# A graph layer's accumulator adds, taken from PSUM through an SBUF copy that ScalarE makes

## The chip, the cores and the metric

One core of one Trainium2 chip. The metric is the device time of one execution in microseconds (us), the median of several runs. Five engines work side by side, each through its own queue in order: TensorE (PE in the profile, its weight loads PEld), VectorE (DVE), ScalarE (ACT), GpSimd (POOL) and SyncE (SP). They meet by semaphores only.

## What is computed

```python
# x (6250, 64); src, dst, edge_type (200000,), edges sorted by dst; weight (16, 64, 64)
h = maximum(layernorm(x), 0)
msg[e] = h[src[e]] @ weight[edge_type[e]]
x + segment_sum(msg, dst, num_segments=6250)
```

## The kernel before

The result is summed in SBUF, transposed, in one wide tile: `accT`, one column for each of the 6250 nodes, the 64 features twice over the 128 partitions (the two halves are added at the very end). Edges are sorted by target, so a stretch of edges touches a window of at most 32 nodes, and its sum is added into 32 columns of `accT` that begin at a base read from the data (`base_row`).

The edges take two ways to a window:

- 125440 of them in 140 groups of 896, worked on two at a time: 70 pairs, n = 0 to 69. For a pair TensorE gathers source rows by products with one-hot matrices (L1264), ScalarE copies the gathered rows from PSUM to SBUF (`take_messages`, L672), and TensorE sums them by relation and target (L1281) into banks 3 and 4. `take_sums` (L681) copies those two banks to `agg`. For every second pair `weigh` (L1308) multiplies the sums of four groups by the 16 weight matrices: 4 windows of 32 columns in one bank, the target bank.
- 74560 of them in 98 stretches of at most 768. GpSimd fetches ready products `h @ weight` from a table in DRAM, and `sum_gathered` (L1324) sums each stretch into 32 more columns of the same target bank.

Batch k (k = 1 to 35) is one filled target bank: 128 columns from `weigh(k - 1)` and 32 for each of its gathered stretches (three in most batches, two in four of them, none in the last). Bank 5 holds odd batches, bank 7 even ones, so a bank is written again two batches later.

`add_sums(k)` on VectorE empties it: a load of four bases into registers (L974), a wait for the weighing (`s_fl`) and for the last gathered sum (`s_sump`), four adds, a load of the other bases (L985), and an add for each gathered stretch, all at L966, each waiting for the one before (`s_add`). It reads the bank where it lies, in PSUM. Before batch k, `weigh` and `sum_gathered` wait until the adds of batch k - 2 are done (`added_by(k - 2)`).

The order is written out by hand. On TensorE a pair has three steps c = 0, 1, 2 (a third of its gathers each), and in each step the gathers come first and then the sums (L1281) of the step before. In step 0 of an even pair n this gives: gathers; the last sums of pair n - 1; gathered stretches; `sort_permute` (L1173). Step 1: gathers; `rank_spilled` (L1181), which waits for `z_sb`; sums of step 0; `weigh` of batch n/2. ScalarE in step 0: `take_messages`, `take_sums(n - 1)`, `take_z` (L615, which fills `z_sb`), and then `take_messages` of step 1. VectorE in pair n: `sort_slots(n + 2)` (L818, L820, L812), `sort_values` (L858), `sort_ranges`, `source_hots` (L936), in even pairs `add_sums(n/2 - 1)`, then `key_hots` (L946) of the next pair, in a ring of 22 buffers that TensorE's sums set free, with `sort_spilled` (L832, L812) and more between them.

After the last pair ScalarE does `take_sums(69)`, TensorE `weigh(34)`, and VectorE, in the branch that is taken when no window overflows, `last_sums`: `add_sums(34)` and `add_sums(35)`. Then it signals `s_done` (L1070), TensorE turns `accT` back (L1387), and VectorE adds the halves and x (L1081).

Of the kernel before, what the change touches and what calls it, by code (L numbers as in the profile page):

```python
# [11 lines left out]
ALU = mybir.AluOpType  # L12
ACT = mybir.ActivationFunctionType
AX = mybir.AxisListType.X
P = 128
EPS = 1e-5
BANK = 512
# [12 lines left out]
def gnn_program(nc, x, src, dst, etype, weight, out):  # L30
# [11 lines left out]
    NS, SJ, SQ, SK, SW, GR = 140, 7, 17, 3, 32, 4  # L42
# [4 lines left out]
    NPR, PT = NS // 2, 2 * SJ  # L47
# [12 lines left out]
    PJ, PW, PRING, PHOTS = 6, 32, 8, 6  # L60
# [114 lines left out]
    for i in range(FETCHES):  # L175
        at = FIRST + (LAST - FIRST) * i / FETCHES
        four = i - len(tile_time)
        spills = four < NGR and starts[2 * four + 1] <= at or len(tile_time) == PALL
        at = max(at, starts[2 * four + 1]) if spills else at
# [14 lines left out]
    batch = [place[m] // 2 for m in range(NP)]  # L194
    batches = [[m for m in range(NP) if batch[m] == k] for k in range(NPR // 2 + 1)]
    adds_of = lambda k: GR * (k >= 1) + len(batches[k])
    added_by = lambda k: sum(adds_of(i) for i in range(k + 1))

    def target_bank(k):
        return ps[(7, 5)[k % 2]]  # L200

    def sum_place(m):
        at = GR * SW + batches[batch[m]].index(m) * PW
        return slice(at, at + PW)
# [18 lines left out]
    sb = lambda name, shape, dt=F32: ctx.enter_context(nc.sbuf_tensor(name, shape, dt))  # L223
    sem = lambda name: ctx.enter_context(nc.semaphore(name))
    with ctx:
# [27 lines left out]
        spreadv = sb("spreadv", [P, PT, 2, SQ], F16)  # L253
        z_sb = sb("z_sb", [P, 3, 2, SQ])
        rel_row = sb("rel_row", [SQ, 2, P], F16)
        iota_key = sb("iota_key", [P, R * SW], F16)
        iota_slot = sb("iota_slot", [P, P], F16)
        iota_range = sb("iota_range", [P, SQ], F16)
# [26 lines left out]
        at = 0  # L285
# [8 lines left out]
        for name in ("src_p", "typ_p", "dst_p"):  # L294
# [48 lines left out]
        s_hot, s_khot, s_gat, s_gev, s_agg, s_aev, s_fl, s_add = (  # L343
            sem(f"s_{n}") for n in ("hot", "khot", "gat", "gev", "agg", "aev", "fl", "add"))
        s_gp = [sem(f"s_gp{k}") for k in range(PRING)]
        s_hotp, s_sump, s_go = sem("s_hotp"), sem("s_sump"), sem("s_go")
        s_over = sem("s_over")
        s_src_b, s_typ_b, s_dst_b, s_nat_b, s_turn_b, s_turned_b, s_base_b, s_row_b = (
            sem(f"s_{n}") for n in ("src_b", "typ_b", "dst_b", "nat_b", "turn_b", "turned_b", "base_b", "row_b"))
        s_done, s_oT, s_half, s_res = sem("s_done"), sem("s_oT"), sem("s_half"), sem("s_res")  # L350
# [208 lines left out]
        def _(act):  # L559
# [58 lines left out]
            def take_rel(g):  # L618
                act.wait_ge(s_relT, g + 1)
                if g >= 2:  # L620
                    act.wait_ge(s_rel[g % 2], 16 * (g // 2))
                act.copy(rel_row[:, g % 2, :], ps[6][0:SQ, 0:P]).then_inc(s_relrow, 1)

            def take_spilled(g):

                act.wait_ge(s_xz, g + 1)
                w = g // 2
                if w >= 2:
                    act.wait_ge(s_xwin, w - 1)
                act.copy(spill_z[:, w % 2, :], ps[6][:, 480:488]).then_inc(s_xzev, 1)  # L630
# [33 lines left out]
            def take_messages(n, c):  # L664
                for b in banks_of(n, c):
                    u = n * GB + b
                    act.wait_ge(s_gat, u + 1)
                    if u >= MB:
                        last_n, last_b = divmod(u - MB, GB)
                        act.wait_ge(s_agg, last_n * SQ + min(2 * last_b + 2, SQ))  # L670
                    width = min(2, SQ - 2 * b)
                    act.copy(msg_s[:, u % MB, 0:width, :].rearrange("p q c -> p (q c)"),  # L672
                             ps[gather_bank(u)][:, 0:width * ROW]).then_inc(s_gev, 1)

            def take_sums(n):
                act.wait_ge(s_agg, (n + 1) * SQ)
                g = n // 2
                if g >= 1:
                    act.wait_ge(s_fl, g)
                for a in range(2):  # L680
                    act.copy(agg[:, n % 2 * 2 + a, :], ps[3 + a][:, :]).then_inc(s_aev, 1)  # L681

            for n, c in STREAM:
                take_messages(n, c)
                if turned(n, c):
                    take_rel(turned(n, c))
                if spilled(n, c) and spilled(n, c) % 2 == 1:
                    take_spilled(spilled(n, c))
                if c == 2 and n in (TURN_AT, KEY_TURN_AT):
                    take_last((TURN_AT, KEY_TURN_AT).index(n))  # L690
                if c == 0 and n >= 1:
                    take_sums(n - 1)
                if permuted(n, c):
                    take_z(permuted(n, c))
            take_sums(NPR - 1)

            def general(act):
                for n, (a, b) in enumerate(gbanks):
# [8 lines left out]
        def _(dve):  # L707
# [249 lines left out]

            def add_sums(k):

                bank = target_bank(k)  # L960

                def add(rows, base, width, at):
                    if added[0]:
                        dve.wait_ge(s_add, added[0])
                    here = accT[rows, bass.ds(base, width)]
                    dve.tensor_tensor(here, here, bank[rows, at], ALU.add).then_inc(s_add, 1)  # L966
                    added[0] += 1

                if k == 1:
                    dve.wait_ge(s_acc0, 8)  # L970
                    dve.wait_ge(s_row_s, 16)
                if (k - 1) * GR == NSA:
                    dve.wait_ge(s_row_b, 16)
                _, bases = nc.values_load_multi_w_load_instructions(  # L974
                    base_row[0:1, (k - 1) * GR:k * GR], engines=[dve.engine], min_val=0, max_val=N,
                    skip_runtime_bounds_check_because="the bases are clamped to it where they are made")
                dve.wait_ge(s_fl, k)
                if batches[k]:
                    dve.wait_ge(s_sump, batches[k][-1] + 1)
                for i, base in enumerate(bases):  # L980
                    add(slice(0, P), base, SW, slice(i * SW, (i + 1) * SW))
                if batches[k]:
                    if batches[k][0] == 0:
                        dve.wait_ge(s_row_p, 16)
                    _, bases = nc.values_load_multi_w_load_instructions(  # L985
                        base_row[0:1, NS + batches[k][0]:NS + batches[k][-1] + 1], engines=[dve.engine], min_val=0, max_val=N,
                        skip_runtime_bounds_check_because="the bases are clamped to it where they are made")
                    for m, base in zip(batches[k], bases):
                        add(slice(0 if len(tiles_of(m)) > 1 else tiles_of(m)[0] % 2 * D, P), base, PW, sum_place(m))
# [12 lines left out]
            for n in range(NPR):  # L1002
# [8 lines left out]
                if n % 2 == 0 and n >= 4:  # L1011
                    add_sums(n // 2 - 1)
# [59 lines left out]
            for g, (a, b) in enumerate(out_groups):  # L1072
                dve.wait_ge(s_oT, g + 1)
                for half in range(2):
                    for i in range(a, b, OB // 2):
                        n = min(b - i, OB // 2)
                        bank = ps[g % 4 * 2 + (i - a) // (OB // 2)][:, 0:n * P].rearrange("p (t h d) -> p t h d", h=2, d=D)
# [9 lines left out]
        def _(pe):  # L1087
# [211 lines left out]
            def weigh(g):  # L1299
                k = g + 1  # L1300
                pe.wait_ge(s_aev, (g + 1) * GR)
                if added_by(k - 2) > 0:
                    pe.wait_ge(s_add, added_by(k - 2))
                pe.wait_ge(s_gx[g % 2], 16 * (g // 2 + 1))
                pe.wait_ge(s_xwin, g + 1)
                for r in range(R):
                    half, first = r % 2, r < 2
                    last = pe.matmul(target_bank(k)[half * D:(half + 1) * D, 0:GR * SW], w_cat[:, r, :], agg[:, :, r * SW:(r + 1) * SW],  # L1308
                                     start=first, stop=r >= R - 2)
                    if r < R - 1:  # L1310
                        spot(last)
                    if r == R // 2 - 1:
                        pe.matmul(target_bank(k)[0:D, 0:GR * SW], msg_x[:, g % 2, :], win_x[:, g % 2, :], start=False, stop=False)
                last.then_inc(s_fl, 1)

            def sum_gathered(m):
                pe.wait_ge(s_hotp, m + 1)
                pe.wait_ge(s_gp[m % PRING], 16 * fetched(m))
                if added_by(batch[m] - 2) > 0:
                    pe.wait_ge(s_add, added_by(batch[m] - 2))  # L1320
                tiles = tiles_of(m)
                for j in tiles:
                    rows, half = rows_of(m, j), j % 2
                    last = pe.matmul(target_bank(batch[m])[half * D:(half + 1) * D, sum_place(m)], msg_p[rows, m % PRING, j, :],  # L1324
                                     hot_p[rows, m % PHOTS, j, :], start=j < tiles[0] + 2, stop=j >= PJ - 2)
                last.then_inc(s_sump, 1)
# [55 lines left out]
            for g, (a, b) in enumerate(out_groups):  # L1382
                if g >= 4:
                    pe.wait_ge(s_res, g - 3)
                for t in range(a, b):
                    bank, i = ps[g % 4 * 2 + (t - a) // (OB // 2)], (t - a) % (OB // 2)
# [17 lines left out]
```

## Time and profile before

| | |
|---|---|
| Time, median of 3 runs | 1066.32 us (1064.34 to 1066.62) |
| Profiled execution, first to last instruction | 1203.7 us |
| TensorE matmuls busy | 1083.9 us (90%) |
| VectorE busy | 938.3 us (78%) |
| GpSimd busy | 682.1 us (57%) |
| ScalarE busy | 450.0 us (37%) |
| Mean granted TensorE clock | 0.984 |

The profiled execution has no time of its own beside its span, and the span is 137.4 us longer than the median without the profiler. So a share of the span is not a share of the time, and TensorE's busy time is by itself more than the median. Durations are read from the profile; differences are added to the median.

In rows of a timeline a group of the same instructions is merged: start, us from the first start to the last end, and the count. In square brackets stands how long the engine was idle before, and who ended that. "remote" and "another core or an unknown queue" are releasers that the profile does not know; "issue" is none at all.

### The profile page before, as it was taken

How to read it: one execution, taken by the hardware profiler on the slowest of the kernel's cores; microseconds unless marked ns; L12 is line 12 of the kernel's file. 1: busy time of each engine (PE TensorE's matmuls, PEld its weight loads, DVE VectorE, ACT ScalarE, POOL GpSimd, SP SyncE). 2: the span in 40 equal slices, each digit the busy share in tenths (PEclk: the TensorE clock that was granted, in tenths of full speed). 3: DMA queues.
4: the chain of work that ended last, by engine and by line, in shares of the span. 5: the costliest groups of instructions: out<-in, count | busy, mean ns of one | idle time of the engine just before them, and what ended most of it. 6: DMA issues, size and time to landing. Idle time of an engine off the chain costs nothing.

```text
span 1203.7 us, 39145 instructions
## 1 busy us (share of the span) xinstructions
PE 1083.9 (90%) x15421; PEld 740.5 (62%) x15421; DVE 938.3 (78%) x2773; ACT 450.0 (37%) x1157; POOL 682.1 (57%) x647
## 2 busy tenths in 40 slices
PE   3998999899989889999999999999999999999897
PEld 1445666666666566666666666666666666666665
DVE  7756878897877688788778778878887887888874
ACT  4884333333333333333333333333333333333332
POOL 2213665566666665667666666666665656666630
PEclk9998999999999899999999999999999999999999
DMA  6795222222222122222222122222222222222211
GB/s 173 301 401 186 59 61 59 58 59 59 62 59 59 37 57 59 59 60 58 59 58 57 43 59 58 60 59 58 60 59 60 59 58 59 58 60 59 59 32 56
DMA packets 41739, 93.69 MB, mean 78 GB/s; under 512 B 14572, under 2 KB 14574, under 8 KB 41557
## 3 DMA queue, kind: packets, MB, share of 16 engines
q1 hardware_dynamic: 13850, 42.12, 10.3%
q0 software_dynamic: 19776, 20.29, 9.9%
q10 hardware_dynamic: 7930, 28.76, 6.2%
q8 instruction: 126, 2.06, 0.7%
q14 instruction: 57, 0.46, 0.1%
HBM read 63.52 MB, written 27.59 MB: 76 GB/s over the span
## 4 chain that ended last, share of the span: by engine, by line
PE 74%; issue 8%; DVE 6%; ACT 5%; another core or an unknown queue 3%; DMA 2%; ACTq 1%; POOL 0%; SPq 0%; DVEq 0%; POOLq 0%
PE ps L1281 33%; PE ps L1264 21%; PE ps L1308 6%; PE ps L1324 3%; ACT u L602 3%; PE ps L1173 3%; DVE u L946 2%; PE ps L1164 2%; PE ps L1197 2%; DMA table<-u 1%; DMA w_cat<-weight 1%; PE ps L1158 1%; PE ps L1203 1%; PE ps L1186 1%
## 5 line engine op out<-in xcount | busy, mean ns | idle before, releaser
L529 POOL DMA_INDIRECT u<-table,row_idx x583 | 612.7, 1051 | 411.3 <-PE ps L1264 138.8
L1281 PE MATMUL ps<-u 64*64 64x512 bf16 (+1 forms) x7280 | 466.5, 377 | 18.0 <-issue 16.0
L672 ACT CAST u<-ps 128x384 bf16<-128x384 f32 (+1 forms) x630 | 265.2, 465 | 527.8 <-PE ps L1264 464.2
L946 DVE TENSOR_SCALAR u<-iota_key,z_sb 128x512 bf16<-128x512 f16 x1190 | 359.9, 368 | 70.3 <-PE ps L1281 50.9
L1264 PE MATMUL ps<-parts,u 128*128 128x192 bf16 x3430 | 333.6, 250 | 11.0 <-issue 9.3
L1281 PEld LDWEIGHTS ps<-u 64*64 64x64 bf16 x7280 | 215.0, 106 | 204.7 <-issue 75.9
L1264 PEld LDWEIGHTS ps<-parts,u 128*128 128x128 bf16 x3430 | 280.6, 99 | 41.0 <-issue 38.5
L936 DVE TENSOR_SCALAR u<-u,node_id 128x1152 bf16<-128x1152 f16 (+2 forms) x420 | 184.5, 495 | 0.0
L681 ACT COPY u<-ps 128x512 f32<-128x512 f32 x140 | 75.2, 589 | 109.5 <-remote 76.8
L966 DVE TENSOR_TENSOR accT<-accT,ps 128x32 f32 x238 | 44.8, 188 | 58.4 <-DVE accT L966 23.1
L1308 PE MATMUL ps<-u,w_cat 128*64 128x128 f32 x1120 | 77.4, 277 | 1.7 <-ACT u L681 1.2
L812 DVE TENSOR_TENSOR u<-iota_slot,rank 128x896 f16<-128x896 f16 x70 | 76.4, 1092 | 2.4
L832 DVE SCALAR_TENSOR_TENSOR spill_rank<-ps,spill_mask 128x14 f32<-128x14 f32 x70 | 11.7, 167 | 84.1 <-issue 30.1
L1308 PEld LDWEIGHTS ps<-u,w_cat 128*64 128x64 f32 x1120 | 65.5, 136 | 15.9 <-issue 14.3
L1324 PE MATMUL ps<-u 128*64 128x32 f32 x1166 | 58.2, 226 | 15.4 <-issue 15.2
L1324 PEld LDWEIGHTS ps<-u 128*64 128x64 f32 x1166 | 46.2, 137 | 38.6 <-issue 37.5
L516 POOL DMA_INDIRECT msg_x<-table,spill_row x35 | 48.2, 1377 | 34.4 <-PE ps L1264 19.2
L1115 PE MATMUL ps<-w_cat,hT 64*128 64x512 f32 x196 | 62.7, 670 | 2.7 <-ACT u L602 2.6
L1173 PE MATMUL ps<-spreadv,u 128*128 128x68 f16 x490 | 30.0, 197 | 27.3 <-DVE spreadv L858 13.2
L602 ACT COPY u<-ps 128x512 f32<-128x512 f32 x98 | 50.7, 604 | 7.6 <-PE ps L1115 3.4
L812 DVE TENSOR_TENSOR spill_hot<-iota_slot,spill_rank 128x448 f16<-128x448 f16 x70 | 43.9, 627 | 2.4
L858 DVE TENSOR_TENSOR spreadv<-ranges,vals 128x476 f16<-128x476 f16 x70 | 45.5, 650 | 0.0
(131 smaller groups left out, 656.4 us busy)
## 6 DMA issues: line engine op xcount, KB each, us to landing
u<-rel_dram SPq DMA_DIRECT2D x70, 544.0 KB
table<-u ACTq DMA_DIRECT2D x24, 1024.0 KB, 5.2
u<-table,row_idx POOLq DMA_INDIRECT x583
rel_dram<-rel_row SPq DMA_DIRECT2D x70, 4.2 KB
x_sb<-x SPq DMA_DIRECT2D x2, 448.0 KB
out<-h_sb SPq DMA_DIRECT2D x3, 224.0 KB
out<-h_sb ACTq DMA_DIRECT2D x3, 224.0 KB
msg_x<-table,spill_row POOLq DMA_INDIRECT x35
```

Of the source, the lines that this page charges most:

```text
L529: pool.indirect_dma_start(out=msg_p[:, b, j, :], out_offset=None, in_=table, in_offset=bass.IndirectOffsetOnAxis(ap=row_idx[:, j, m:m + 1] ...
L602: act.copy(t_out[:, i % TRING, t, half * BANK:(half + 1) * BANK], ps[piece_bank(k)][:, :]).then_inc(s_tev, 1)
L672: act.copy(msg_s[:, u % MB, 0:width, :].rearrange("p q c -> p (q c)"), ps[gather_bank(u)][:, 0:width * ROW]).then_inc(s_gev, 1)
L681: act.copy(agg[:, n % 2 * 2 + a, :], ps[3 + a][:, :]).then_inc(s_aev, 1)
L812: return dve.tensor_tensor(there, places, mine, ALU.is_equal)
L936: last = dve.tensor_scalar(hot[:, part % HRING, k, 0:(there - low) * P], bc[:, b, low * P:there * P], node_id[:, k:k + 1], None, ALU.is_equal)
L946: dve.tensor_scalar(khot[:, v % KR, :], iota_key[:, :], z_sb[:, n % 3, 1, q:q + 1], None, ALU.is_equal).then_inc(s_khot, 1)
L1173: last = pe.matmul(ps[6][:, 0:4 * SQ].rearrange("p (a c) -> p a c", a=2), slot_hot[:, j, :], values[:, :, j, :], start=j == 0, stop=j == S ...
L1264: last = pe.matmul(there, hot[:, part % HRING, t - q * SK, at * P:(at + 1) * P], parts[:, t, :], start=t == blocks[0], stop=t == blocks[-1])
L1281: last = pe.matmul(ps[3 + a][half * D:(half + 1) * D, keys], msg_s[rows, u % MB, q % 2, part * D:(part + 1) * D], khot[rows, v % KR, keys] ...
L1308: last = pe.matmul(target_bank(k)[half * D:(half + 1) * D, 0:GR * SW], w_cat[:, r, :], agg[:, :, r * SW:(r + 1) * SW], start=first, stop=r ...
L1324: last = pe.matmul(target_bank(batch[m])[half * D:(half + 1) * D, sum_place(m)], msg_p[rows, m % PRING, j, :], hot_p[rows, m % PHOTS, j, : ...
```

## The change

ScalarE gets `take_targets(k)`: it waits for the weighing and for the gathered sums of batch k and for VectorE's adds of batch k - 2, and copies the used columns of the target bank to a new SBUF tile with two halves, `target_sb`. It stands behind `take_sums(n - 1)` in even pairs from n = 4 on, ahead of `take_z`, and twice at the end. `add_sums` waits for that copy (`s_kept`) alone and reads `target_sb`. `weigh` and `sum_gathered` wait for the copy of batch k - 2, no longer for its adds.

```diff
+        target_sb = sb("target_sb", [P, 2, BANK])
...
+            def take_targets(k):
+
+                act.wait_ge(s_fl, k)
+                if batches[k]:
+                    act.wait_ge(s_sump, batches[k][-1] + 1)
+                if added_by(k - 2) > 0:
+                    act.wait_ge(s_add, added_by(k - 2))
+                width = GR * SW + len(batches[k]) * PW
+                act.copy(target_sb[:, k % 2, 0:width], target_bank(k)[:, 0:width]).then_inc(s_kept, 1)
...
                 if c == 0 and n >= 1:
                     take_sums(n - 1)
+                    if n % 2 == 0 and n >= 4:
+                        take_targets(n // 2 - 1)
                 if permuted(n, c):
                     take_z(permuted(n, c))
             take_sums(NPR - 1)
+            take_targets(NPR // 2 - 1)
+            take_targets(NPR // 2)
...
-                bank = target_bank(k)
+                kept = target_sb[:, k % 2, :]
...
-                    dve.tensor_tensor(here, here, bank[rows, at], ALU.add).then_inc(s_add, 1)
+                    dve.tensor_tensor(here, here, kept[rows, at], ALU.add).then_inc(s_add, 1)
...
-                dve.wait_ge(s_fl, k)
-                if batches[k]:
-                    dve.wait_ge(s_sump, batches[k][-1] + 1)
+                dve.wait_ge(s_kept, k)
...
             def weigh(g):
                 k = g + 1
                 pe.wait_ge(s_aev, (g + 1) * GR)
-                if added_by(k - 2) > 0:
-                    pe.wait_ge(s_add, added_by(k - 2))
+                if k > 2:
+                    pe.wait_ge(s_kept, k - 2)
...
-                if added_by(batch[m] - 2) > 0:
-                    pe.wait_ge(s_add, added_by(batch[m] - 2))
+                if batch[m] > 2:
+                    pe.wait_ge(s_kept, batch[m] - 2)
```

What ScalarE has in a row in step 0 of an even pair, before. L672 copies gathered rows, L681 is `take_sums`, L615 `take_z` (line numbers of after are 2 higher up to here):

```order
L672 CAST u<-ps 128x384 [waits s_agg,s_gat] x3
L681 COPY u<-ps 128x512 [waits s_fl,s_agg]
L681 COPY u<-ps 128x512
L615 COPY z_sb<-ps 64x34 [waits s_relT,s_khot,s_z]
L615 COPY z_sb<-ps 64x34
L672 CAST u<-ps 128x384 [waits s_agg,s_gat] x3
```

And now:

```order
L674 CAST u<-ps 128x384 [waits s_agg,s_gat] x3
L683 COPY u<-ps 128x512 [waits s_fl,s_agg]
L683 COPY u<-ps 128x512
L693 COPY target_sb<-ps 128x224 [waits s_add,s_sump,s_fl]
L617 COPY z_sb<-ps 64x34 [waits s_relT,s_khot,s_z]
L617 COPY z_sb<-ps 64x34
L674 CAST u<-ps 128x384 [waits s_agg,s_gat] x3
```

The copy, of 224 columns here (30 of the 35 have 224, four have 192, the last has 128), stands between `take_sums` and `take_z`; nothing else moved.

ScalarE's end, after the gathers of the last pair, before:

```order
L672 CAST u<-ps 128x384 [waits s_agg,s_gat] x5
L672 CAST u<-ps 128x192 [waits s_agg,s_gat]
L681 COPY u<-ps 128x512 [waits s_fl,s_agg]
L681 COPY u<-ps 128x512
L363 TENSOR_LOAD flag_int [waits s_flag]
```

And now:

```order
L674 CAST u<-ps 128x384 [waits s_agg,s_gat] x5
L674 CAST u<-ps 128x192 [waits s_agg,s_gat]
L683 COPY u<-ps 128x512 [waits s_fl,s_agg]
L683 COPY u<-ps 128x512
L693 COPY target_sb<-ps 128x224 [waits s_add,s_sump,s_fl]
L693 COPY target_sb<-ps 128x128 [waits s_add,s_fl]
L365 TENSOR_LOAD flag_int [waits s_flag]
```

Both last copies stand behind the last `take_sums`; the load of the flag follows them.

VectorE's end, before: the last three adds of batch 34, the load of the bases of batch 35, and its first adds, which wait for the weighing.

```order
L985 TENSOR_LOAD base_row
L966 ISA [waits s_add]
L966 TENSOR_TENSOR accT<-accT,ps 128x32
L966 ISA [waits s_add]
L966 TENSOR_TENSOR accT<-accT,ps 128x32
L966 ISA [waits s_add]
L966 TENSOR_TENSOR accT<-accT,ps 64x32
L974 TENSOR_LOAD base_row
L966 ISA [waits s_add,s_fl]
L966 TENSOR_TENSOR accT<-accT,ps 128x32
```

And now:

```order
L999 TENSOR_LOAD base_row
L982 ISA [waits s_add]
L982 TENSOR_TENSOR accT<-accT,target_sb 128x32
L982 ISA [waits s_add]
L982 TENSOR_TENSOR accT<-accT,target_sb 128x32
L982 ISA [waits s_add]
L982 TENSOR_TENSOR accT<-accT,target_sb 64x32
L990 TENSOR_LOAD base_row
L982 ISA [waits s_add,s_kept]
L982 TENSOR_TENSOR accT<-accT,target_sb 128x32
```

The order is the same; the adds of batch 35 wait for ScalarE's copy, and so do those of batch 34 above them (`s_kept` in place of `s_fl` and `s_sump`).

## Rows read from the trace of the kernel before

**Rows 1.** The page's busy times: us, share of the span, instructions.

```profile
PE 1083.9 (90%) x15421; PEld 740.5 (62%) x15421; DVE 938.3 (78%) x2773; ACT 450.0 (37%) x1157; POOL 682.1 (57%) x647
```

**Rows 2.** The page's chain that ended last, by engine.

```profile
PE 74%; issue 8%; DVE 6%; ACT 5%; another core or an unknown queue 3%; DMA 2%; ACTq 1%; POOL 0%; SPq 0%; DVEq 0%; POOLq 0%
```

**Rows 3.** Groups by line, columns: busy us, mean ns; idle us before, releasers.

```profile
L966 DVE TENSOR_TENSOR accT<-accT,ps 128x32 f32 x238 | 44.8, 188 | 58.4 <-DVE accT L966 23.1 <-PE ps L1308 8.5 <-issue 2.6
L1308 PE MATMUL ps<-u,w_cat 128*64 128x128 f32 x1120 | 77.4, 277 | 1.7 <-ACT u L681 1.2 <-issue 0.3
```

**Rows 4.** The same view, shapes apart: ScalarE's copies from PSUM.

```profile
L681 ACT COPY u<-ps 128x512 f32<-128x512 f32 x140 | 75.2, 589 | 109.5 <-remote 76.8 <-PE ps L1281 32.5
L595 ACT COPY hT<-ps 128x128 f32<-128x128 f32 x24 | 6.6, 278 | 9.9 <-PE ps L1115 6.1 <-PE ps L1109 3.7
```

**Rows 5.** The same view, VectorE: a PSUM operand, then SBUF operands alone.

```profile
L818 DVE TENSOR_TENSOR ranks<-ps,ranges 128x238 f32<-128x238 f32 x70 | 27.8, 397 | 14.0 <-PE ps L1164 10.6 <-remote 2.9 <-DVE win_x L848 0.2
L842 DVE TENSOR_TENSOR spill_terms<-spill_z,spill_coef 128x16 f32<-128x16 f32 x35 | 6.1, 174 | 13.7 <-issue 8.5 <-ACT spill_z L630 5.0
L847 DVE CAST spill_row<-spill_sum 128x1 int32<-128x1 f32 x35 | 5.4, 153 | 1.2
```

**Rows 6.** Timeline of ScalarE, step 0 of an even pair: start, us, what.

```profile
638.39 1.07 ACT L681 COPY u<-ps 128x512 f32<-128x512 f32 x2 [1.96 <-remote]
639.35 0.40 ACT L615 COPY z_sb<-ps 64x34 f32<-64x34 f32 x2
639.77 1.24 ACT L672 CAST u<-ps 128x384 bf16<-128x384 f32 x3
```

**Rows 7.** TensorE in the same place: the last gathers, and who waits.

```profile
639.16 0.33 PE L1264 MATMUL ps<-parts,u 128*128 128x192 bf16 x2 [0.22 <-issue]
639.80 0.18 PE L1181 MATMUL ps<-spill_mask,tri 128*128 128x14 f16 x1 [0.31 <-ACT z_sb L615]
```

**Rows 8.** Waits: TensorE for z_sb, in all 70 pairs: us, times, longest.

```profile
PEld ps L1181 <- ACT z_sb L615: 19.2, 29, 1.2
PE ps L1181 <- ACT z_sb L615: 11.1, 22, 1.0
```

**Rows 9.** Timeline of ScalarE, the even pair before: the same two lines.

```profile
606.81 1.07 ACT L681 COPY u<-ps 128x512 f32<-128x512 f32 x2 [2.06 <-remote]
607.77 0.39 ACT L615 COPY z_sb<-ps 64x34 f32<-64x34 f32 x2
```

**Rows 10.** Timeline of VectorE from there to its next sort.

```profile
607.69 1.14 DVE L966 TENSOR_TENSOR accT<-accT,ps 128x32 f32 x4
609.57 0.83 DVE L966 TENSOR_TENSOR accT<-accT,ps 128x32 f32 x3 [0.73 <-DVE accT L966]
...
611.84 0.63 DVE L812 TENSOR_TENSOR spill_hot<-iota_slot,spill_rank 128x448 f16<-128x448 f16 x1
...
617.76 1.81 DVE L946 TENSOR_SCALAR u<-iota_key,z_sb 128x512 bf16<-128x512 f16 x6 [2.29 <-PE ps L1281]
```

**Rows 11.** TensorE there: end of the gathers in step 1; next gathers; spill_hot's reader.

```profile
608.65 0.17 PE L1181 MATMUL ps<-spill_mask,tri 128*128 128x14 f16 x1
...
613.48 1.25 PE L1264 MATMUL ps<-parts,u 128*128 128x192 bf16 x13
614.65 0.38 PE L1197 MATMUL ps<-vals,spill_hot 128*64 128x8 f16 x7
```

**Rows 12.** Timeline of VectorE's end: batch 34, and then batch 35.

```profile
1178.22 0.51 DVE L966 TENSOR_TENSOR accT<-accT,ps 128x32 f32 x2 [2.49 <-PE ps L1324]
...
1181.36 0.19 DVE L966 TENSOR_TENSOR accT<-accT,ps 64x32 f32 x1 [0.16 <-DVE accT L966]
1190.06 1.15 DVE L966 TENSOR_TENSOR accT<-accT,ps 128x32 f32 x4 [8.51 <-PE ps L1308]
```

**Rows 13.** The other engines there, in order of time.

```profile
1186.60 1.07 ACT L681 COPY u<-ps 128x512 f32<-128x512 f32 x2 [3.08 <-PE ps L1281]
...
1188.82 1.09 PE L1308 MATMUL ps<-u,w_cat 128*64 128x128 f32 x15
```


## What the change should do to the time

> **What bounds the kernel now.** Four views, in this order. The busy times [rows 1]: TensorE's matmuls 90% of the span, VectorE 78%, ScalarE 37%. The chain that ended last [rows 2] runs through TensorE for 74%, VectorE 6%, ScalarE 5%. So TensorE sets the pace, and VectorE is near: its 938.3 us are 88% of the 1066.32 us that an execution takes without the profiler. The groups by line [rows 3] show what the change touches: 238 adds of 188 ns, 44.8 us, and idle time before them of 58.4 us, of which 23.1 is one add waiting for another (register loads lie between) and 8.5 the last batch waiting for the weighing. No wait of an add for the weighing or the gathered sums shows in the loop. `weigh` was idle for 1.7 us in all, and for no add of VectorE. So the wait of TensorE that the change shortens, for batch k - 2, holds nobody up today: by the order of work it lies two even pairs back. The last views are timelines of step 0 of an even pair and of the end.
>
> **The copy's size.** A copy of 512 fp32 columns from PSUM takes 589 ns on ScalarE, one of 128 takes 278 [rows 4]: 0.81 ns a column. One of 224 then takes some 356 ns. Behind another copy it adds less: two of 512 end after 1.07 us [rows 6], so the second adds 0.48, and one of 224 columns adds 0.48 - 288 x 0.81 = 0.25 us. 35 copies are some 12 us on an engine that is busy for 450 of 1203.7. ScalarE's own waits in it are over when it comes there: the weighing of the batch and all its gathered sums stand ahead of this pair's gathers on TensorE, and VectorE's adds of batch k - 2 two even pairs back.
>
> **Who stands behind the copy on ScalarE.** First `take_z`, and for that TensorE waits (L1181). [Rows 6, 7] show an even pair in which this is tight: `take_sums` 638.39 to 639.46, z from 639.35 to 639.75, TensorE goes on at 639.80 after 0.31 us of waiting. Put 0.25 us between the first two and TensorE is 0.25 us later. [Rows 9, 11] show the pair before: z ends at 608.16, TensorE comes at 608.65, and the 0.25 us are covered. I went through the 32 even pairs in which the loop has both: in 7 (the first at 165.3, the last at 1012.9) it is as in [rows 6, 7]; in 7 others z directly follows `take_sums`, but TensorE is over 0.4 us later; in the rest z waits for `sort_permute` on TensorE or comes long before it is wanted, so that the copy fits in ahead or goes unseen. 7 x 0.25 = **1.7 us** on TensorE's path. Ends: nothing, if TensorE is always later than z, and 32 x 0.36 = 11.5 us if every pair is tight and the copies don't overlap. I take 1.7, since it is counted. How often TensorE waits for z in all 70 pairs [rows 8] (29 and 22 times, 30.3 us) says that this edge is sharp. Next in ScalarE's queue are the copies of step 1's gathers; TensorE wants those banks again at 613.48 [rows 11], 4 us after they are free, so nothing comes of it.
>
> **What VectorE loses.** (a) The adds. Nothing makes them shorter. A two-tensor operation with a PSUM operand takes 397 ns for 238 columns [rows 5] and 188 for 32 [rows 3], so 1.01 ns a column; one with SBUF operands alone takes 174 for 16 columns [rows 5], and 16 columns more make it 190. 238 x 2 ns is 0.5 us, on an engine with slack. The Trainium skill (VectorE: DVE Perf Modes, the section on the TRN2 errata) has a table in which an operation from PSUM has 62 cycles more of fixed cost than one from SBUF; by it the adds would be 65 ns shorter, 15 us in all. The same section says that a fixed term of some 150 cycles is what was measured for fp32 adds from SBUF; these rows side with that. (b) The wait. Before, adds began as soon as VectorE came to them. Now they need the copy: the end of `take_sums`, 0.25 us for the copy, and 0.15 from one engine to the next (as from TensorE's end at 1189.91 to the add at 1190.06 [rows 12, 13]). In [rows 9, 10] `take_sums` ends at 607.88 and the adds began at 607.69: now 608.28, 0.59 us later. Over the 33 batches in the loop the same sum gives a wait in 21, 15.2 us together, at most 1.9. Behind it in VectorE's queue are the key matrices of the next pair and the sort of spilled edges. The latter's product is at 612.47 and is wanted at 614.65 [rows 10, 11]: 2.2 us of cover. Then VectorE stands still for 2.29 us, until TensorE frees a buffer of the ring [rows 10]. Such a gap before its next sort follows in all but two of these batches, as long as the new wait or within 0.1 us of it. So in this trace the wait is hidden: **0**. Ends: 0 and 15.2 us.
>
> **The end of the program.** Here nothing hides it. Before, batch 34 is added from 1178.22 to 1181.55, under TensorE's last work, VectorE then waits 8.51 us, and batch 35 is added from 1190.06 to 1191.21 [rows 12]. Now the copy of batch 34 stands behind the last `take_sums`, which ends at 1187.67 [rows 13]. Copy: 1187.92; first add: 1188.07. Seven adds with the register load between take 2.71 us in the loop [rows 10]: 1190.78. The load of batch 35's bases, hidden in the 8.51 us so far, takes the 0.73 that such a load shows [rows 10]: 1191.51. The copy of batch 35 is no limit: weighing ends at 1189.91 [rows 13], plus 0.28 and 0.15 is 1190.34. Four adds, 1.15: 1192.66, against 1191.21. **1.45 us**. Ends: 0.7 if the load overlaps the adds before it, 2.1 if batch 34 takes the 3.33 us that it took in [rows 12].
>
> **Sum.** 1.7 + 0 + 1.45 = 3.1 us, and no gain against it. On the median: 1066.32 + 3.1 = **1069.4 us**. The profiled span is 137 us longer than that median, but the terms are lengths of instructions on ScalarE and VectorE and a count of tight places; the count is what may differ without the profiler. Something under 0.2% (2.1 us) can't be told from no change here.
>
> **Rivals.**
> A, only the end counts. In half the even pairs `take_sums` begins some 2 us after the sums that it needs, released by something the profile doesn't know [rows 6, 9]. If that is due to the profiler, ScalarE is earlier in a timed run, z waits for `sort_permute` instead, and the copy costs TensorE nothing. Against it: TensorE is quicker too. The time is 1066.3 + 1.45 = 1067.8, no change that can be told.
> B, VectorE's wait comes through. It holds if VectorE has no slack left in a timed run, which its 88% suggests [rows 1]. Against it: a VectorE that is late comes to the adds after the copy, and then there is no wait. Half of 15.2 with the 3.1 gives 1077.
> C, faster: VectorE is what the timed run waits for, and the adds do get shorter. The floor for an operation from SBUF is the 153 ns of a one-column cast [rows 5]: 35 ns less for each of 238 is 8.3 us. With the end's 1.45 that is 1059.5. It decides for faster from (2.1 + 1.45) / 238 = 15 ns an add. The slope above speaks against it. The table of the Trainium skill named above points this way.
> That the change does nothing is excluded: the new order has the copies and the waits on both sides.
>
> **Chances.** As worked out (1068 to 1072): 0.42, of it 0.07 under 2.1 us. A: 0.27. B: 0.15. C: 0.07. Other: 0.09, a third each way. That makes slower 0.35 + 0.15 + 0.03 = 0.53, same 0.07 + 0.27 + 0.03 = 0.37, faster 0.07 + 0.03 = 0.10. The range leaves out C and the far half of B: 1065 to 1076.5.
>
> **What would show it.** In the profile of after: 35 copies of about 356 ns; TensorE's idle time at `rank_spilled`, for z, up by about 2 us; adds of 188 to 191 ns; idle time before the loop's adds up by about 15 us, for ScalarE's copy, and idle time of the key matrices, for TensorE, down by as much; the last add ending some 2.7 us after TensorE's last weighing matmul, where it was 1.3 [rows 12, 13]. I am wrong if the adds are under 175 ns, if TensorE's idle time for VectorE's sorts (L1173) rises, or if batch 34 at the end is not added behind the last `take_sums`.

## The result

The median of 20 runs is 1067.61 us (1065.09 to 1070.41), against 1065.62 us (1063.58 to 1068.45) for 20 runs of the kernel before. The ratio is 1.0022, with a 95% interval of 1.0011 to 1.0032: 2.3 us slower, between 1.2 and 3.4. (The ratio is not that of the two medians, which lie 2.0 us apart; here and below the microseconds come from the ratio.) Forecast were 3.1 us, 1069.4 us in all; the time lies in the range of 1065 to 1076.5, and just under the 1068 to 1072 of the case as it was worked out.

One thing must be said ahead of the profile. Its span is 1068.1 us, where that of before was 1203.7 us. This is not the change's doing. The runs were on several chips, on which the kernel before takes 1065, 1181 to 1183 and 1199 us *without* the profiler. By its span the profile of before comes from a chip of the long kind (over 1180 us); the times of before come from one of the short kind (1065 us). The prediction took the difference for the profiler's. That it is the chip and not its host, say, was not tested. So the two profiles can't be laid side by side in the loop; in the end they can, since nothing waits there for what is late on the long chips. For the loop the experiments give the profile that is wanted: one kernel whose loop is that of before, on the short kind.

The page of after, its busy times (us, share of the span, instructions), as [rows 1], and its chain, as [rows 2]:

```profile
PE 1010.9 (95%) x15421; PEld 709.7 (66%) x15421; DVE 937.4 (88%) x2773; ACT 469.7 (44%) x1192; POOL 687.2 (64%) x647
...
PE 63%; DVE 22%; issue 7%; ACT 4%; DMA 3%; DVEq 1%; ACTq 1%; POOL 0%; SPq 0%; POOLq 0%
```

VectorE's busy time is what it was, in a span 136 us shorter, and it now holds 22% of the chain. The groups by line (busy us, mean ns, idle us before, releasers), as [rows 3, 4]:

```profile
L982 DVE TENSOR_TENSOR accT<-accT,target_sb 128x32 f32 x238 | 45.9, 193 | 61.3 <-DVE accT L982 24.9 <-ACT target_sb L693 13.5 <-issue 1.1
L683 ACT COPY u<-ps 128x512 f32<-128x512 f32 x140 | 75.2, 589 | 91.4 <-PE ps L1295 91.4
```

238 adds of 193 ns in place of 188: not shorter, but 5 ns longer. They wait 13.5 us for ScalarE's copy, but in the list of waits (us, times, longest) this is nearly one wait, of 12.9 us, at the end; and TensorE hardly waits for z, against [rows 8]:

```profile
DVE accT L982 <- ACT target_sb L693: 13.5, 2, 12.9
...
PEld ps L1195 <- ACT z_sb L617: 1.5, 2, 0.8
```

The copies themselves (duration ns least, median, most):

```profile
L693 ACT COPY target_sb<-ps x35: 266/363/365, 159.6 to 1051.9; 128x224 f32<-128x224 f32 x30, 128x192 f32<-128x192 f32 x4, 128x128 f32<-128x128 f32 x1
```

An even pair of the loop, timeline of all engines with lines left out (start, us, what), against [rows 6, 7, 10]:

```profile
625.29 1.07 ACT L683 COPY u<-ps 128x512 f32<-128x512 f32 x2 [1.28 <-PE ps L1295]
...
626.25 0.36 ACT L693 COPY target_sb<-ps 128x224 f32<-128x224 f32 x1
626.49 0.40 ACT L617 COPY z_sb<-ps 64x34 f32<-64x34 f32 x2
...
627.46 0.51 DVE L982 TENSOR_TENSOR accT<-accT,target_sb 128x32 f32 x2
627.66 0.17 PE L1195 MATMUL ps<-spill_mask,tri 128*128 128x14 f16 x1
```

The copy does push z back, by 0.25 us, as counted. But z is there at 626.89 and TensorE comes for it at 627.66; and the copy is there at 626.61 and VectorE comes for it at 627.46. Both engines are later than ScalarE, in this pair and in nearly all others: by the lists of waits TensorE waits for z twice, and VectorE for the copy once beside the wait at the end. ScalarE's idle time ahead of `take_sums` ends on TensorE's sums here, where it ended on something unknown in [rows 6, 9].

And the end, against [rows 12, 13]:

```profile
1048.53 1.07 ACT L683 COPY u<-ps 128x512 f32<-128x512 f32 x2 [3.08 <-PE ps L1295]
1049.49 0.36 ACT L693 COPY target_sb<-ps 128x224 f32<-128x224 f32 x1
...
1049.99 0.52 DVE L982 TENSOR_TENSOR accT<-accT,target_sb 128x32 f32 x2 [12.92 <-ACT target_sb L693]
...
1050.75 1.09 PE L1322 MATMUL ps<-u,w_cat 128*64 128x128 f32 x15
1051.01 0.52 DVE L982 TENSOR_TENSOR accT<-accT,target_sb 128x32 f32 x2 [0.50 <-DVE accT L982]
1051.89 0.27 ACT L693 COPY target_sb<-ps 128x128 f32<-128x128 f32 x1 [2.03 <-PE ps L1322]
1052.25 0.52 DVE L982 TENSOR_TENSOR accT<-accT,target_sb 128x32 f32 x2 [0.72 <-DVE accT L982]
1052.92 0.19 DVE L982 TENSOR_TENSOR accT<-accT,target_sb 64x32 f32 x1 [0.16 <-DVE accT L982]
1053.51 1.16 DVE L982 TENSOR_TENSOR accT<-accT,target_sb 128x32 f32 x4 [0.40 <-DVE accT L982]
...
1054.75 7.58 PE L1401 MATMUL ps<-ident,accT 128*128 128x128 f32 x49 [2.91 <-DVE excess_max L1084]
1056.77 0.76 DVE L1095 TENSOR_TENSOR h_sb<-ps,x_sb 128x256 f32<-128x256 f32 x2 [2.09 <-PE ps L1401]
```

Batch 34 is added from 1049.99 on, behind the last `take_sums`, where before it began at 1178.22, 8.4 us ahead of the last `take_sums` [rows 12, 13]. Batch 35's copy is done at 1052.16; its adds begin at 1053.51, since they stand behind those of batch 34. The last add ends at 1054.67, 2.83 us after the last weighing (1051.84). Before it was 1191.21 - 1189.91 = 1.30 us. That is 1.53 us lost.

There is a second loss that the prediction did not have. The 49 transposes behind take 7.58 us, where the same 49 before take

```profile
1191.29 6.33 PE L1387 MATMUL ps<-ident,accT 128*128 128x128 f32 x49 [1.38 <-DVE excess_max L1070]
```

and VectorE gets the first banks after 2.09 us of idle time in place of 1.36. The stretches of 4 us that begin 0.5 us before (busy us and instructions of PE, PEld, DVE, ACT, POOL, then the granted clock; before is the first):

```profile
1190.70:1194.70 4.00, 3.41 (x27) 3.41 (x28) 2.51 (x10) 0.00 (x0) 0.00 (x0) 1.00 0.01 4
```

```profile
1054.20:1058.20 4.00, 3.45 (x18) 3.45 (x19) 1.77 (x7) 0.00 (x0) 0.00 (x0) 0.57 0.01 4
```

18 matmuls in place of 27, at a granted clock of 0.57 in place of 1.00: for most of that stretch the clock was at its lower level, 1.2 GHz in place of 2.4. TensorE had been idle for 2.91 us there, and for 1.38 before. From the last add to the end of the program it is 1203.7 - 1191.21 = 12.5 us before and 1068.1 - 1054.67 = 13.4 now: 0.9 us. Together 2.5 us, close to the 2.3 measured.

### The profile page after: what moved, and what is told of

Same layout as the page of the kernel before. It is cut to its first block, busy times and chain, and to the rows that moved or that the text cites. A ratio compares the mean times of both kernels' runs of the same rounds, so it can differ in the third digit from the quotient of the medians.

```text
span 1068.1 us, 39214 instructions
## 1 busy us (share of the span) xinstructions
PE 1010.9 (95%) x15421; PEld 709.7 (66%) x15421; DVE 937.4 (88%) x2773; ACT 469.7 (44%) x1192; POOL 687.2 (64%) x647
## 4 chain that ended last, share of the span: by engine, by line
PE 63%; DVE 22%; issue 7%; ACT 4%; DMA 3%; DVEq 1%; ACTq 1%; POOL 0%; SPq 0%; POOLq 0%
PE ps L1295 27%; PE ps L1278 19%; DVE u L962 10%; PE ps L1322 5%; ACT u L604 3%; DVE u L952 3%; PE ps L1187 2%; PE ps L1338 2%; DVE spreadv L874 2%; PE ps L1211 1%; DMA table<-u 1%; PE ps L1129 1%; DVE rank L836 1%; DMA w_cat<-weight 1%; PE ps L1178 1%
## 5 line engine op out<-in xcount | busy, mean ns | idle before, releaser
L531 POOL DMA_INDIRECT u<-table,row_idx x583 | 629.2, 1079 | 273.9 <-issue 121.4
L674 ACT CAST u<-ps 128x384 bf16<-128x384 f32 (+1 forms) x630 | 281.8, 462 | 436.7 <-PE ps L1278 426.7
L1295 PE MATMUL ps<-u 64*64 64x512 bf16 (+1 forms) x7280 | 425.9, 375 | 0.0
L962 DVE TENSOR_SCALAR u<-iota_key,z_sb 128x512 bf16<-128x512 f16 x1190 | 367.0, 377 | 10.4 <-PE ps L1295 6.9
L1278 PE MATMUL ps<-parts,u 128*128 128x192 bf16 x3430 | 319.4, 247 | 0.5 <-ACT key_p L594 0.5
L1295 PEld LDWEIGHTS ps<-u 64*64 64x64 bf16 x7280 | 194.2, 106 | 159.9 <-issue 11.2
L982 DVE TENSOR_TENSOR accT<-accT,target_sb 128x32 f32 x238 | 45.9, 193 | 61.3 <-DVE accT L982 24.9
L518 POOL DMA_INDIRECT msg_x<-table,spill_row x35 | 37.1, 1061 | 27.5 <-PE ps L1278 19.7
L1338 PE MATMUL ps<-u 128*64 128x32 f32 x1166 | 47.2, 225 | 0.0
L1187 PE MATMUL ps<-spreadv,u 128*128 128x68 f16 x490 | 26.9, 195 | 21.4 <-DVE spreadv L874 20.4
L1129 PEld LDWEIGHTS ps<-w_cat,hT 64*128 64x128 f32 x196 | 27.4, 202 | 20.2 <-ACT u L604 12.0
```

The costliest lines, as they stand in the source:

```text
L531: pool.indirect_dma_start(out=msg_p[:, b, j, :], out_offset=None, in_=table, in_offset=bass.IndirectOffsetOnAxis(ap=row_idx[:, j, m:m + 1] ...
L962: dve.tensor_scalar(khot[:, v % KR, :], iota_key[:, :], z_sb[:, n % 3, 1, q:q + 1], None, ALU.is_equal).then_inc(s_khot, 1)
L1129: last = pe.matmul(bank[:, :], hT[t * D:(t + 1) * D, i % 2, :], w_cat[t * D:(t + 1) * D, half * R // 2:(half + 1) * R // 2, :].rearrange(" ...
L1278: last = pe.matmul(there, hot[:, part % HRING, t - q * SK, at * P:(at + 1) * P], parts[:, t, :], start=t == blocks[0], stop=t == blocks[-1])
L1295: last = pe.matmul(ps[3 + a][half * D:(half + 1) * D, keys], msg_s[rows, u % MB, q % 2, part * D:(part + 1) * D], khot[rows, v % KR, keys] ...
```

## Experiments

The first four ran on one chip, of the short kind (the kernel before: 1065.43 us, median of 35 runs).

**The end alone.** The kernel before, with `target_sb`, `s_kept` and `take_targets` as in the change, used for batches 34 and 35 only.

```diff
             take_sums(NPR - 1)
+            take_targets(NPR // 2 - 1)
+            take_targets(NPR // 2)
...
-                bank = target_bank(k)
+                copied = k >= NPR // 2 - 1
+                bank = target_sb[:, k % 2, :] if copied else target_bank(k)
```

> The kernel before, with ScalarE's copies for batches 34 and 35 alone. Theory (the whole loss is at the end: the last add 1.5 us later, and TensorE's transposes behind it slower by 0.75 us since TensorE stood idle for 2.9 us in place of 1.4): +2.3 us, a ratio of 1.002, the same as the whole change. Rival (the loop pays too, through adds of 193 ns in place of 188 and the wait for the copy): at most +1.5 us here, and the rest in the kernel that has the loop's copies alone.

Measured: 1067.98 us, ratio 1.0026 (1.0013 to 1.0039), +2.8 us. Two of 35 copies cost what all of them cost, within the noise. This profile has the loop of before on a chip of the short kind, so it is the one to compare the loop with. Its adds, by line:

```profile
L981 DVE TENSOR_TENSOR accT<-accT,ps 128x32 f32 x227 | 42.5, 187 | 45.0 <-DVE accT L981 23.0 <-issue 1.1
```

And the loop from 105 to 1040 us (columns as in the stretches above):

```profile
105.00:1040.00 935.00, 914.79 (x14895) 657.56 (x14897) 855.42 (x2597) 390.75 (x1005) 663.68 (x618) 1.00 0.25 65
```

The windows view of after gives 913.53 for TensorE and 856.76 for VectorE in the same 935 us. That is how busy the loops are; how long they are can be read from the first and the last start of TensorE's gathers, here and then in after (duration ns least, median, most):

```profile
L1282 PE MATMUL ps<-parts,u x3430: 242/246/368, 103.0 to 1042.9; 128*128 128x192 bf16 x191
```

```profile
L1278 PE MATMUL ps<-parts,u x3430: 242/246/368, 105.1 to 1044.5; 128*128 128x192 bf16 x191
```

939.9 us without the loop's copies and 939.4 with them: the loops are alike. What differs by 2.1 us is where the gathers begin, ahead of the first copy (159.6 us); with the change in the kernel it is anywhere from 102.4 to 105.1 us. TensorE waits for z 1.5 us here as well. Its waits for VectorE's sorts, whose growth the prediction had named as a sign of being wrong, are 19.6 and 11.9 us here, 20.4 and 12.0 in after.

**The loop alone.** The change, but batches 34 and 35 are added from PSUM as before.

```diff
-            take_targets(NPR // 2 - 1)
-            take_targets(NPR // 2)
...
-                kept = target_sb[:, k % 2, :]
+                copied = k < NPR // 2 - 1
+                kept = target_sb[:, k % 2, :] if copied else target_bank(k)
```

> The change with batches 34 and 35 added from PSUM as before; the other 33 go through the copies. Theory: within 0.5 us of before (33 batches whose adds take 2.72 us in place of 2.71, ScalarE's copy unseen). Rival (VectorE is full, so that 5 ns for each of 227 adds is 1.1 us): +1 to +1.5 us.

Measured: 1065.81 us, ratio 1.0007 (0.9995 to 1.0019): +0.7 us, between -0.5 and +2.0. The 33 copies of the loop cost nothing that is clear of noise, though the rival's 1.1 us of longer adds can't be excluded by the time. In the profile the gathers go from 104.9 to 1044.3 us, 939.4 us once more. The adds, by line:

```profile
L981 DVE TENSOR_TENSOR accT<-accT,target_sb 128x32 f32 x227 | 43.6, 192 | 45.9 <-DVE accT L981 23.2 <-issue 1.1 <-ACT target_sb L693 0.6
```

The transposes at the end, in the timeline:

```profile
1052.97 6.33 PE L1405 MATMUL ps<-ident,accT 128*128 128x128 f32 x49 [1.38 <-DVE excess_max L1088]
```

In 33 batches VectorE waits for the copy once, 0.6 us, and the transposes take 6.33 us again.

**Batch 34 first.** The change, with one line moved.

```diff
-            take_sums(NPR - 1)
             take_targets(NPR // 2 - 1)
+            take_sums(NPR - 1)
             take_targets(NPR // 2)
```

> The change, with the copy of batch 34 ahead of the last take_sums in place of behind it. Theory: the last add ends 0.5 us later than before in place of 1.5, TensorE's idle time ahead of its transposes is 1.9 us, and the time is +0.5 us if its clock stays up, +1.2 if it falls. Rival (loss in the loop): the time stays at +2 us or over.

Measured: 1066.79 us, ratio 1.0014 (1.0005 to 1.0023): +1.5 us, between 0.5 and 2.5. The trace:

```profile
1048.33 1.09 PE L1322 MATMUL ps<-u,w_cat 128*64 128x128 f32 x15
1049.47 0.27 ACT L693 COPY target_sb<-ps 128x128 f32<-128x128 f32 x1 [2.29 <-PE ps L1322]
1049.86 1.16 DVE L982 TENSOR_TENSOR accT<-accT,target_sb 128x32 f32 x4 [3.34 <-ACT target_sb L693]
...
1051.11 6.33 PE L1401 MATMUL ps<-ident,accT 128*128 128x128 f32 x49 [1.69 <-DVE excess_max L1084]
```

The last add ends 1.60 us after the weighing (1.30 before, 2.83 in the change), TensorE is idle for 1.69 us, and its clock stays up (1.00 in the 4 us from 0.5 us before the transposes). Only batch 35's own copy is left on the path. The interval of the time holds both the theory's 0.5 us and the rival's 2; it is the trace that decides.

**TensorE kept busy.** The change, and between the last weighing and the wait for `s_done`:

```diff
+            for i in range(14):
+                pe.transpose(ps[0][:, 0:P], ident[:, :], ident[:, :])
             pe.wait_ge(s_done, 1)
```

> The change, with 14 transposes of the identity into a free bank after TensorE's last weighing, so that it isn't idle for over a microsecond before the last transposes. Theory: the granted clock stays at 1.0 there, the first eight transposes take 1.3 us as before and the time is 0.75 us less than the change's: +1.5 us on before. Rival (the clock's fall costs nothing): +2.3 us.

Measured: 1067.04 us, ratio 1.0018 (1.0008 to 1.0029): +1.9 us. The timeline:

```profile
1050.57 1.16 DVE L982 TENSOR_TENSOR accT<-accT,target_sb 128x32 f32 x4 [0.40 <-DVE accT L982]
...
1051.81 6.33 PE L1403 MATMUL ps<-ident,accT 128*128 128x128 f32 x49 [1.23 <-DVE excess_max L1084]
```

The 4 us from 1050.4 on, with the granted clock:

```profile
1050.40:1054.40 4.00, 2.77 (x23) 2.59 (x22) 2.07 (x9) 0.00 (x0) 0.00 (x0) 1.00 0.02 4
```

The adds are as late as in the change, and yet the transposes take 6.33 us at a clock of 1.00: it was the idle time, not the late adds, that took the clock down. As a time the 0.4 us between this kernel and the change (1.9 against 2.3) isn't clear of noise; that the clock does this is shown by the trace, that it costs 0.9 us of the time is not, by itself.

What carries it is the whole row of kernels. From the end of the last weighing to the end of the program (span less the time at which it ends), against the time measured:

| kernel | last weighing to end | against before | time against before |
|---|---|---|---|
| before | 1203.7 - 1189.9 = 13.8 | | |
| loop alone | 1065.4 - 1051.6 = 13.8 | 0.0 | +0.7 (-0.5 to 2.0) |
| batch 34 first | 1063.5 - 1049.4 = 14.1 | 0.3 | +1.5 (0.5 to 2.5) |
| TensorE kept busy | 1064.3 - 1048.9 = 15.4 | 1.6 | +1.9 (0.9 to 3.1) |
| the change | 1068.1 - 1051.8 = 16.3 | 2.5 | +2.3 (1.2 to 3.4) |
| end alone | 1066.3 - 1050.2 = 16.1 | 2.3 | +2.8 (1.4 to 4.2) |

The times lie in the order of the ends but for the last two, and each interval holds the difference of the ends, but for batch 34 first, which is 0.2 us outside.

**The kernel before, profiled again.**

> The kernel before, unchanged, profiled again. Expected: a span near 1066 us, without ScalarE's idle stretches that end on an unknown releaser; VectorE 88% busy, with little idle time in the loop; TensorE waiting for VectorE's sorts (L1173) and hardly for z (L1181); adds of 188 ns. If the stretched profile was the usual one, all this stays as it was, with a span near 1200 us.

It met a chip of the long kind: one run of 1202.51 us, where that chip's other runs of the same kernel had a median of 1198.78. The span is 1200.8 us, and the waits are those of the first profile:

```profile
ACT u L681 <- remote: 73.3, 28, 3.8
...
DVE u L946 <- PE ps L1281: 53.7, 54, 2.6
```

So the stretch isn't the profiler's. The expectation's first guess was wrong, and so was the prediction's.

**Adds from SBUF.** The kernel before, with another operand in the loop's adds.

```diff
-                    dve.tensor_tensor(here, here, bank[rows, at], ALU.add).then_inc(s_add, 1)
+                    dve.tensor_tensor(here, here, (w_flat if k < NPR // 2 - 1 else bank)[rows, at], ALU.add).then_inc(s_add, 1)
```

> The kernel before, but the adds of batches 1 to 33 take a tile that lies in SBUF all along (the weights) in place of the target bank, with the same waits; no copy, no new wait. So it adds something else to the accumulator. Theory: adds of 192 to 193 ns in place of 188, which is 1.1 us of VectorE's time in all; the time moves by 0 to 1.1 us. Rival (an operand in SBUF makes VectorE's adds shorter): 174 ns or less, and a time 2 us or more below before.

Measured, on the same long chip: ratio 0.9996 (0.9980 to 1.0013). The operand alone makes the adds longer:

```profile
L967 DVE TENSOR_TENSOR accT<-accT,w_cat 128x32 f32 x227 | 43.9, 193 | 44.9 <-DVE accT L967 18.4 <-issue 5.4
```

193 ns, where both the kernel before and the eleven adds left in PSUM here take 188 to 189; on the chip of the short kind it was 192 against 187. So rival C of the prediction has no ground: what matters is the place of the tile, without any copy, and an operand in SBUF makes the adds longer, not shorter. The time says little here, since VectorE has slack on this chip.

**More work on VectorE.** The kernel before, with this ahead of each batch's adds in the loop:

```diff
+                if k < NPR // 2 - 1:
+                    for i in range(4):
+                        dve.tensor_tensor(spare[:, i, :], iota_own[:, i * SW:(i + 1) * SW], iota_win[:, :], ALU.add)
```

> The kernel before, with four more small two-tensor operations (128x32, SBUF to SBUF) on VectorE in each of 33 batches, ahead of the adds: 132 of 190 ns. Theory (VectorE paces the loop without the profiler's delays, together with TensorE): +10 to +25 us. Rival (TensorE alone sets the pace and VectorE's time is covered, as the stretched trace had it): under 2 us.

Measured: ratio 0.9995 (0.9974 to 1.0017) on the chip of 1199 us: the rival's side, on this chip. By line:

```profile
L983 DVE TENSOR_TENSOR spare<-iota_own,iota_win 128x32 f32<-128x32 f32 x132 | 16.3, 185 | 0.0
```

Since they overlap one another, 132 operations of 185 ns are 16.3 us and not 25, so the work added was less than the expectation counted on. Again:

> The same kernel as e6_more_vector_work, 132 more small operations on VectorE. In the earlier comparison the kernel before took 1199 us on the chip in use, not 1065, and nothing moved the time. If this one meets a chip on which the kernel before takes 1065 us: +10 to +25 us if VectorE paces the loop with TensorE there, under 2 us if not. On a chip of 1199 us: no change again, since VectorE has slack there.

Measured on the chip of 1181 us: ratio 1.0028 (1.0014 to 1.0042), +3.3 us. VectorE's busy time is 947.0 us there and 939.0 in the change on such a chip; it may be that a part of the extra work shows in the time here, where on the chip of 1199 us none did (busy 951.0 against 937.0). This chip is neither of the two that the expectation named, so whether VectorE paces the loop on a chip of 1065 us stays untested.

**The adds on GpSimd.** With the sums in `target_sb`, in SBUF, another engine can take the adds. Batches 1 to 33 go to it, one add between two of its fetches; batches 34 and 35 stay on VectorE, from PSUM.

```diff
+            def add_one():
...
+                _, (base,) = nc.values_load_multi_w_load_instructions(
+                    base_row[0:1, at:at + 1], engines=[pool.engine], min_val=0, max_val=N,
...
+                here = accT[:, bass.ds(base, SW)]
+                pool.tensor_tensor(here, here, target_sb[:, k % 2, i * SW:(i + 1) * SW], ALU.add).then_inc(s_add, 1)
```

> What the copy to SBUF makes possible: GpSimd does the adds of batches 1 to 33 from target_sb, one between two of its fetches, each with its own load of the base; VectorE keeps batches 34 and 35, from PSUM. Theory (VectorE is full, and 33 times 2.7 us leave it): the time falls by 10 to 40 us, if GpSimd (64% busy) keeps its fetches in time. Rival (VectorE isn't what the loop waits for): no change, or slower because the gathered rows come late.

> The same kernel as e8_adds_on_gpsimd. On a chip on which the kernel before takes 1065 us: 10 to 40 us less, if VectorE paces the loop there and GpSimd keeps its fetches in time; no change or more if not. On a chip of 1199 us: no change again.

> The adds of batches 1 to 33 on GpSimd, a third time, beside the change. On a chip of 1065 us: 10 to 40 us less than before if VectorE paces the loop there; on one of 1181 or 1199 us: within 0.3% of before, as twice.

Measured: 1.0009 (0.9992 to 1.0026) at 1199 us, 1.0019 (1.0004 to 1.0034) at 1181, 1.0027 (1.0007 to 1.0046) at 1183. No gain there, and in the last two a loss of 2.2 and 3.2 us. The loss isn't at the end: from the last weighing to the end of the program it is 13.9 us in the last one (1184.7 - 1170.8), as before. Its cause stays open. In the last of them GpSimd takes 305 ns for an add, and VectorE's time for the adds mostly turned into time spent waiting for TensorE's sums (30.0 us in the change on the same chip, below). By line, and then in the list of waits:

```profile
L547 POOL TENSOR_TENSOR accT<-accT,target_sb 128x32 f32 x227 | 69.3, 305 | 5.5 <-POOL accT L547 1.4
```

```profile
DVE u L994 <- PE ps L1333: 101.9, 61, 4.0
```

This kernel was never on a chip of the short kind, where VectorE waits little for those sums (6.9 us in after). Whether it is faster there stays open.

**The change again**, on the chip of 1182.54 us.

> The change itself, once more, whatever chip it meets. Theory (the loss is 1.5 us up to the last add and 0.75 us of slower transposes behind it, on no engine that has slack): +2.3 us on a chip of 1199 or 1181 us as well, where VectorE waits in the loop. Rival (where TensorE and ScalarE are late, the copy ahead of z costs TensorE up to 1.7 us more): +4 us there.

Measured: ratio 1.0014 (1.0000 to 1.0028): +1.7 us, between 0 and 3.3 (the medians lie 2.6 us apart). The rival's +4 is outside. This profile can be laid beside that of before in the loop, nearly; the chips differ by 1.4%. Its waits, and then the transposes by line:

```profile
DVE u L962 <- PE ps L1295: 30.0, 53, 2.6
...
PEld ps L1195 <- ACT z_sb L617: 18.1, 30, 1.2
DVE accT L982 <- ACT target_sb L693: 16.8, 7, 12.5
```

```profile
L1401 PE MATMUL ps<-ident,accT 128*128 128x128 f32 x49 | 7.8, 333 | 2.9 <-DVE excess_max L1084 2.9
```

Here VectorE does wait for the copy in the loop, 16.8 - 12.5 = 4.3 us in six batches by this list (the group's whole idle time is 70.9 us, 12.5 more than in [rows 3], part of it at the end), and its idle time before the key matrices is 30.0 us, against 53.7 in the profile above. But that is a chip of 1199 us; the kernel with more work on VectorE, without any copy, has 29.2 us on the chip of 1181, so how much of the difference is the copy's isn't shown. TensorE's wait for z is 18.1 us, against 19.2 in [rows 8] and 21.0 in the second profile of before; since those two differ by as much as the 1.7 us looked for, it is the time, not this wait, that speaks against the rival. At the end TensorE is idle for 2.9 us once more, and the transposes take 7.8 us. From the last weighing (1168.85) to the end (1185.1) it is 16.3 us, as in the change on the short chip.

## Why the prediction came out as it did

The sign, the mechanism at the end and the range were right. That the sum of 3.1 us came so near the 2.3 measured is luck: a term of 1.7 us was in it that was nothing, and one of 0.9 us was missing.

- **The end, 1.45 us.** Right to a tenth: 1.53, of which moving one copy ahead took back 1.23. Each step can be read in the trace: the copy behind `take_sums`, the first add 0.39 us after it (0.40 counted), batch 35 in line behind batch 34. Only the inner gaps were other than taken, and they nearly cancel: 3.12 us for batch 34 in place of 2.71, and 0.40 for the load in place of 0.73.
- **What was missing.** The sum ended with the last add. The engine that then takes over had been idle for twice as long, and its clock was down: 0.9 us more. The prediction took the work behind the last add to be as long as before, without a reason; the 49 transposes there took 7.58 us in place of 6.33.
- **TensorE's wait for z, 1.7 us.** Nothing: 1.5 us of such waiting in all the program, in after as well as in the kernel with the loop of before. The count of seven tight pairs was right for its trace, but that trace is of a chip on which ScalarE starts `take_sums` late (76.8 us of waiting for an unknown releaser [rows 4], none in after). The prediction had this as rival A ("only the end counts"), with 0.27, and as for the mechanism that rival is what happened; with the clock's share it came to 2.3 us, not to 1.45. Rival A blamed the profiler for the late starts, which is wrong: it goes with the chip. On a chip of the long kind the 1.7 us on top of the end's 2.3 to 2.5 would be some 4 us, and the second comparison of the change has 3.3 at most.
- **VectorE's wait, 0 us.** Right as to the time, but not by the way forecast. The waits of 15.2 us in 21 batches did not come: 4.3 us in six batches on the long chip, 0.6 us in one on the short one. That the key matrices' idle time hid them isn't shown. On the short chip there was hardly a wait to hide, for the reason given against rival B: a VectorE that is late comes after the copy. Rival B itself, a loss in the loop, did not happen: the loop alone is +0.7 us, 2.0 at most.
- **The adds.** Forecast 2 ns longer, measured 5, and up to 1.1 us of VectorE's time, which may be the 0.7 us of the loop alone. The table of the Trainium skill (VectorE: DVE Perf Modes, the section on the TRN2 errata) would have had them 65 ns shorter, an estimate that this case does not bear out; the formula in the same section for fp32 adds from SBUF, with a fixed term of 151 cycles, gives an estimate of 191 ns for 32 columns, and these measured 192 to 193.
- **TensorE's waits on the copy of batch k - 2.** As forecast, in no profile does `weigh` or `sum_gathered` wait for it.

## What to carry over

A copy that frees a bank early is worth something only if somebody waits for the bank; here nobody did, and the one place where the copy had no cover, the end of the program, set the price. In a queue that is written by hand, look at what is put *behind* a late instruction though its own data are long there: moving one line ahead took the last add from 2.83 to 1.60 us after the weighing. And compare the profiled span with the timed runs before counting tight places in it: where they differ by 13%, as here, a count of near misses and the time may belong to two different chips.

## What the chip did that was not expected

- TensorE's clock at the end. After 1.23, 1.38 and 1.69 us without a matmul the last transposes ran at a granted clock of 1.00 and took 6.33 us; after 2.71 and 2.91 us they ran at 0.57 in the 4 us around their start and took 7.63 and 7.58 us, and after 2.91 us on the chip of 1183 us at 0.62, and took 7.75. The window for the kernel with the end alone:

```profile
1052.40:1056.40 4.00, 3.46 (x17) 3.46 (x18) 1.75 (x7) 0.00 (x0) 0.00 (x0) 0.57 0.02 4
```

- Chips differ: 1065, 1181 to 1183 and 1199 us for the same kernel. On the long ones TensorE's matmuls are busy for 1071 to 1084 us in place of 1007 to 1011; ahead of the weight loads for the sums TensorE stands still in 214 short gaps, 75.9 us in all, that end on nothing in the profile (profile of before), against 71 gaps and 11.2 us in after; and ScalarE and GpSimd wait for an unknown releaser. VectorE's busy time is nearly the same on both, 937 to 939 us. What is slower there was not found out.
- An operand in SBUF made a 128x32 fp32 add longer, 192 to 193 ns against 187 to 188 from PSUM.
